# A hand-ordered drain for the last stage of a two-layer decoder, with the last softmax shares spread by TensorE and ScalarE

## The reference

```python
def _L1_xattn_ref(x, latents, mask, g1, b1, g2, b2, Wq, Wkv, Wout):
    xn, ln_lat = layer_norm(x, g1, b1), layer_norm(latents, g2, b2)
    q = ln_lat @ Wq
    k, v = jnp.split(jnp.concatenate([xn, ln_lat], axis=1) @ Wkv, 2, axis=-1)
    weight = einsum('bhld,bhnd->bhln', q * scale, k * scale)   # masked
    return to_rows(einsum('bhln,bhnd->bhld', softmax(weight), v)) @ Wout

def bitlinear(x, norm_w, w):
    x_norm = rmsnorm(x, norm_w)
    return einsum('bsd,hd->bsh', activation_quant(x_norm), weight_quant(w))

def _L1_ffn_ref(x, norm1_w, w1, act_scale, act_bias, norm2_w, w2):
    h = act_scale * square(relu(bitlinear(x, norm1_w, w1))) + act_bias
    return bitlinear(h, norm2_w, w2)

x = _layernorm(x + _L1_xattn_ref(ctx, x, mask, ...))
x = _layernorm(x + _L1_ffn_ref(x, ...))
```

## Time and profile before

| | us |
|---|---|
| median of 3 runs | 1576.4 |
| lowest, highest | 1575.58, 1577.85 |
| the profiled execution | 1580.26 |
| its span | 1578.4 |
| last score exponent (step 63) starts at | 1501.55 |
| TensorE busy over the span | 1415.3 (90%) |
| VectorE busy | 1132.3 (72%) |
| ScalarE busy | 959.6 (61%) |
| GpSimd busy | 306.6 (19%) |

### The profile page before, as it was taken

How to read it: one execution, slowest core, us unless ns; L and a number is a source line. 1 busy time by engine, 2 the same in 40 slices (tenths; PEclk the granted TensorE clock), 3 DMA queues, 4 the chain that set the end, 5 groups by cost and what they waited for, 6 DMA issues and landing times. The chain is left out here.

```text
span 1578.4 us, 32271 instructions
## 1 busy us (share of the span) xinstructions
PE 1415.3 (90%) x12643; PEld 868.5 (55%) x12658; DVE 1132.3 (72%) x2367; ACT 959.6 (61%) x1494; POOL 306.6 (19%) x278
## 2 busy tenths in 40 slices
PE   6999999998999888888898778999999999999962
PEld 4666666665665334434444354666666666666541
DVE  4666778885435799999999744455667767776787
ACT  2333367766555988899888843456555556555433
POOL 3433344542001101111010021121111111110011
PEclk9999999998999999999999999999999999999985
DMA  4000000000100000000000012222222222222310
GB/s 182 2 2 2 2 19 12 15 6 8 49 1 1 1 1 1 1 1 1 1 1 4 1 27 62 65 58 63 63 65 67 67 64 60 58 58 61 72 43 17
DMA packets 41013, 50.78 MB, mean 32 GB/s; under 512 B 9248, under 2 KB 23200, under 8 KB 40480
## 3 DMA queue, kind: packets, MB, share of 16 engines
q1 hardware_dynamic: 40576, 48.06, 11.9%
q10 hardware_dynamic: 288, 0.67, 0.1%
HBM read 13.04 MB, written 2.10 MB: 10 GB/s over the span
## 5 line engine op out<-in xcount | busy, mean ns | idle before, releaser
L1852 DVE TENSOR_TENSOR l_px<-psum,l_share 128x1024 f32<-128x1024 f32 x64 | 78.4, 1225 | 158.9 <-PE psum L1554 104.9
L1702 ACT ACTIVATE l_prob<-psum,l_bias 128x1024 f32<-128x1024 f32 x64 | 71.3, 1114 | 175.9 <-PE psum L1529 175.9
L1541 PE MATMUL psum<-l_XT,l_A 128*128 128x256 f32 x512 | 127.2, 393 | 1.5 <-ACT l_XT L1720 1.5
L1524 PE MATMUL psum<-l_th,l_XT 128*128 128x512 f32 x256 | 125.4, 613 | 1.5 <-DVE stream L1859 0.9
L1592 PE MATMUL psum<-l_px,l_N 128*128 128x256 f32 x512 | 124.8, 387 | 1.8 <-ACT l_r L1746 1.8
L1554 PE MATMUL psum<-l_prob,l_X 128*128 128x512 f32 x256 | 123.2, 604 | 0.0
L1592 PEld LDWEIGHTS psum<-l_px,l_N 128*128 128x128 f32 x512 | 94.6, 192 | 19.2 <-issue 4.7
L1833 DVE TENSOR_REDUCE l_top<-psum 128x8 bf16<-128x1024 f32 x64 | 78.1, 1221 | 36.4 <-PE psum L1609 36.4
L1541 PEld LDWEIGHTS psum<-l_XT,l_A 128*128 128x128 f32 x512 | 94.7, 194 | 12.6 <-ACT l_XT L1720 1.7
L1266 DVE TENSOR_TENSOR f_frac<-psum,f_whole 128x1024 f32<-128x1024 f32 x80 | 98.0, 1225 | 2.7
L1258 DVE TENSOR_SCALAR f_whole<-psum 128x1024 f32<-128x1024 f32 x80 | 97.5, 1218 | 1.6 <-PE psum L895 1.6
(11 more groups left out here) (310 smaller groups left out, 3216.2 us busy)
## 6 DMA issues: line engine op xcount, KB each, us to landing
l_share<-l_recip SPq DMA_DIRECT2D x512, 64.0 KB, 2.0
early_weights<-in_weights SPq DMA_DIRECT2D x1, 2405.0 KB, 11.4
c_cs<-in_ctx SPq DMA_DIRECT2D x16, 128.0 KB, 2.1
f_qf<-in_l_mats SPq DMA_DIRECT2D x1, 2048.0 KB, 8.0
out<-l_normed SPq DMA_DIRECT2D x16, 128.0 KB, 2.0
l_craw<-in_ctx SPq DMA_DIRECT2D x15, 128.0 KB, 2.3
late_weights<-in_weights SPq DMA_DIRECT2D x1, 1089.0 KB, 11.2
relbias<-in_relbias ACTq DMA_DIRECT2D x1, 512.0 KB, 5.2
```

Source lines behind the costliest of these rows:

```text
L1524: nc.tensor.matmul(ps[:, SC + n, :], XT[:, q % 3, k, :, :], th[:, q % 2, k, 8 * n:8 * n + 8, :], start=True, stop=False)
L1541: last = nc.tensor.matmul(ps[:, at + j // 2, (j % 2) * 256:(j % 2 + 1) * 256], A[:, QB * k + j, :], XT[:, q % 3, :, 1, :], start=True, sto ...
L1852: nc.vector.tensor_tensor(px[:, q % 2, :, k, :], ps[:, GA:GA + 2, :].rearrange("p a (h s) -> p (a h) s", s=S), share[:, (b // 2) % 2, b % ...
```

## The change

- Every engine's loop now stops at step 63 (`range(FIRST, B)`), and what followed is written as a list of calls, one quad at a time, in an order of its own on each engine.
- The last pair's shares (sequences 62 and 63) come no more by 16 DMAs. PE multiplies a column block of ones (`one_row`, one row of ones in each block of 32 partitions) by `recip`, four matmuls of 32 rows and 512 columns into banks 0 to 3 (`spread_last`), and ACT copies the banks into `share` (`keep_last_shares`).
- POOL's `normed_hidden` of quads 12 to 15 becomes a DVE product (`last_products`). DVE's `scaled_hidden` of these quads becomes an ACT pass (`last_scaled`). The two scale-and-add passes L1881 of the hidden values of quads 11 to 15 become two ACT passes (`last_lifted`). Quad 13's to 15's tokens keep theirs on DVE, but the tiny scale steps come apart from them.
- ACT's `measure` writes its unused squares into two idle buffers instead of `r`, so `r` is free sooner.
- Banks change: `hidden` of quads 13 to 15 goes to GA, the turned tokens to RO, the last quad's combine and turn-back to RO + 1, the gather of sequence 63 to RO. `deq2` has two copies.
- At the start of the phase DVE sets `one_row` with five memsets.

The core of the diff:

```diff
-            for i in range(FIRST, LAST):
+            for i in range(FIRST, B):
...
+            def spread_last():
+                pe.wait_ge(s["one_row"], 2)
+                pe.wait_ge(s["recip"], B // 2)
+                for n in range(4):
+                    rows = slice(32 * n, 32 * n + 32)
+                    last = nc.tensor.matmul(ps[:, (RO, RO + 1, SC, SC + 1)[n], :], one_row[rows, :], recip[rows, 1, :], start=True, stop=True)
+                last.then_inc(s["wide_ps"], 1)
...
+            def keep_last_shares():
+                act.wait_ge(s["wide_ps"], 1)
+                act.wait_ge(s["px_sb"], B - 4)
+                for b in range(2):
+                    at = (RO, SC)[b]
+                    nc.scalar.copy(share[:, 1, b, :, :], ps[:, at:at + 2, :]).then_inc(s["last_share"], 1)
...
+            def last_scaled(q):
+                act.wait_ge(s["squared"], q + 1)
+                act.wait_ge(s["hn"], q)
+                act.wait_ge(s["ss2"], q)
+                nc.scalar.activation(hh[:, :, :], r[:, :, :], ACT.Identity, scale=w("b_as"), bias=w("b_ab")).then_inc(s["hh"], 1)
+
+            def last_lifted(q):
+                act.wait_ge(s["hscaled"], q - OLD + 1)
+                for t in range(TQ):
+                    last = nc.scalar.activation(hn[:, t, :], hn[:, t, :], ACT.Copy, scale=hscale[:, t:t + 1], bias=MAGIC)
+                last.then_inc(s["hlifted"], 1)
...
+            def last_products(q):
+                dve.wait_ge(s["hh"], q + 1)
+                dve.wait_ge(s["q_ready"], q)
+                nc.vector.tensor_tensor(hn[:, :, :], hh[:, :, :], w("b_n2").unsqueeze(1).to_broadcast([P, TQ, HID]), ALU.mult
+                                        ).then_inc(s["hn"], 1)
...
+            def last_quantised(q):
+                dve.wait_ge(s["hlifted"], q - OLD + 1)
+                dve.wait_ge(s["q_ps"], TQ * q)
+                nc.vector.tensor_scalar(hi[:, :, :], hn[:, :, :], MAGIC, 127.0, ALU.subtract, ALU.min).then_inc(s["q_ready"], 1)
+                nc.vector.tensor_scalar(deq2[:, q % 2, :], amax2[:, :], 1.0 / 127.0, wmean[:, 1:2], ALU.mult, ALU.mult)
...
+            hidden_biggest(Q - 5)
+            divide(B - 3)
+            invert(B // 2 - 1)
+            last_scales(Q - 5)
+            tokens(Q - 3)
+            last_token_scales(Q - 3)
+            last_quantised(Q - 5)
+            divide(B - 2)
+            last_products(Q - 4)
...
```

More of the change, by code:

```diff
@@ new lines, in last_hidden_turned @@
+            def last_hidden_turned(q):
+                pe.wait_ge(s["q_ready"], q + 1)
+                pe.wait_ge(s["hiT_sb"], TQ * q)
+                pe.wait_ge(s["last_share"], 2)
+                for t in range(TQ):
+                    for n in range(HC):
+                        last = nc.tensor.matmul(ps[:, SC + t, n * P:(n + 1) * P], hi[:, t, n * P:(n + 1) * P], ident16[:, :],
+                                                start=True, stop=True)
+                    last.then_inc(s["q_ps"], 1)
@@ new lines, in last_down @@
+            def last_down(q):
+                pe.wait_ge(s["d_read"], q)
+                pe.wait_ge(s["sums_read"], B // 2)
+                down(q)
+            gather(B - 3)
+            pe.wait_ge(s["d_read"], Q - 5)
+            sums(B // 2 - 1)
+            hidden(Q - 4)
+            gather(B - 2)
+            pe.wait_ge(s["r_sb"], TQ * (Q - 3))
+            spread_last()
+            combine(Q - 2, 1)
+            combine(Q - 2, 2)
+            combine(Q - 2, 3)
+            gather(B - 1)
@@ new lines, in last_measure, with root1, root2 @@
+            def last_measure(q):
+                act.wait_ge(s["hh"], q + 1)
+                act.wait_ge(s["hscaled"], q - OLD)
+                act.wait_ge(s["staged"], Q - 1)
+                act.wait_ge(s["ss2"], q)
+                for t in range(TQ):
+                    last = nc.scalar.activation(junk[t], hh[:, t, :], ACT.Square, accum_out=ss2[:, t:t + 1])
+                last.then_inc(s["ss2"], 1)
+            def root1(q):
+                roots_of(q, None, None)
+            def root2(q):
+                roots_of(None, q, None)
@@ new lines, in last_tokens_quantised @@
+            def last_tokens_quantised(q):
+                dve.wait_ge(s["x_ps"], q)
+                for t in range(TQ):
+                    last = nc.vector.tensor_scalar(xn[:, t, :], xn[:, t, :], xscale[:, t:t + 1], MAGIC, ALU.mult, ALU.add)
+                step(last)
+                nc.vector.tensor_scalar(xi[:, :, :], xn[:, :, :], MAGIC, 127.0, ALU.subtract, ALU.min).then_inc(s["x_ready"], 1)
+                dve.wait_ge(s["r_sb"], TQ * q)
+                nc.vector.tensor_scalar(deq[:, :], amax[:, :], 1.0 / 127.0, wmean[:, 0:1], ALU.mult, ALU.mult).then_inc(s["deq1"], 1)
@@ new lines, in _ @@
+            divide(B - 2)
+            last_products(Q - 4)
+            hidden_biggest(Q - 4)
+            last_scales(Q - 4)
+            divide(B - 1)
+            last_tokens_quantised(Q - 3)
+            last_quantised(Q - 4)
+            last_residual(Q - 2)
+            residual_moments(Q - 2)
+            normalise(Q - 6)
+            tokens(Q - 2)
+            last_token_scales(Q - 2)
+            last_tokens_quantised(Q - 2)
+            last_products(Q - 3)
+            hidden_biggest(Q - 3)
@@ new lines, in _ @@
+            last_residual(Q - 1)
+            last_scales(Q - 3)
+            residual_moments(Q - 1)
+            down_read(Q - 5)
+            tokens(Q - 1)
+            last_token_scales(Q - 1)
+            last_tokens_quantised(Q - 1)
+            down_moments(Q - 5)
+            last_quantised(Q - 3)
+            last_products(Q - 2)
+            hidden_biggest(Q - 2)
+            normalise(Q - 5)
+            last_scales(Q - 2)
+            down_read(Q - 4)
+            down_moments(Q - 4)
```

197 lines of the change are left out of this document (179 added, 18 removed).

## The result

| | before | after |
|---|---|---|
| median, us | 1575.99 (4 runs, 1573.63 to 1577.85) | **1556.38** (4 runs, 1554.97 to 1560.69) |
| profiled execution, us | 1580.26 | 1560.69 |
| last score exponent starts at | 1501.55 | 1501.98 |
| last normalisation on DVE ends at | 1576.12 | 1556.60 |
| **drain**, the difference of these two | 74.57 | **54.62** |

The ratio of the times, estimated over all runs, is 0.9886, with a 95% interval of 0.9856 to 0.9916; the two medians alone give 0.9876. The profiled executions differ by 19.57 us and the medians by 19.61 (the profiled execution is one of the four runs after, but not one of the four before). The drain alone is 19.95 us shorter; it began 0.43 us later.

A forecast was written before the change was run, and what follows sets the result against it. DVE's 73.1 us queue after the last score bounds the drain: its 63.7 us of work becomes 53.1, plus 0.6 of waits, 19.4 us earlier. With 1.0 friction, net 18.4 less: median 1558.0, range 1555.5 to 1565.5.

The forecast's parts named there:

- A: Drain: DVE bounds it without gaps, each wait having a named cover; 1558.0 us, chance 0.70.
- POOL leaves: Drain, quads 10 to 13: DVE's normalisation passes fall from 2.66 to 0.60 us without POOL; 8.2 us less.
- The product: Drain: four hidden products come to DVE at 1.22 us plus 0.04 for the reduction's wait; 5.0 us more.
- Scaling and lifts: Drain: four scalings (2.9 us) and five quads' scale-and-add passes (4.5 us) leave DVE for ACT, hidden in its idle time.
- The spread: Last shares: four PE matmuls together take about 1.1 us, and DVE's 3.6 us wait for the DMAs goes.
- rival B: Mid-drain: PE falls to its lower clock and stays; 1564.7 us, or 1566.2 with the spread in turn; chance 0.20.
- Waits of 0.6 us for roots: End of drain: quads 14 and 15 each make DVE wait about 0.3 us for ACT's root.
- Friction: Drain: 1.0 us added for five margins below half a microsecond, at 0.2 us each.
- Tiny steps: DVE's drain: scale steps stay as many, quad 11's `hidden_biggest` only moves ahead of a `divide`; no effect.
- C: Drain: ACT becomes late from 12.6 us of added passes; 1559.8 us, or 1564.2 with slower lifts; chance 0.07.
- D: Drain: ACT's passes hold DVE as POOL's do, 28.4 us, making it slower at 1586.4 us; chance 0.01.
- E: Drain: no gain, from a new in-order block or table loads around ACT's roots; 1577.2 us at most; chance 0.02.

The follow-up runs named there:

- e1: Changed kernel with the hidden product of quads 12 to 15 back on POOL; drain 58.29 us (+3.67 to the change), median 1558.00 us.
- e12: Changed kernel with product on POOL, last shares by 16 DMAs, scaling and lifts on DVE, keeping order, banks, buffers; drain 68.60 us (-5.97 to before).
- e3: Changed kernel with scaling of quads 12 to 15 and lifts of quads 11 to 15 back on DVE; drain 62.34 us (+7.72 to the change).
- e2: Changed kernel with the last pair's shares by 16 DMAs again, without PE's spread and ACT's copies; drain 58.78 us (+4.16 to the change).
- e8: Changed kernel with one more unused 128x512 ACT pass before the scaling of each of quads 12 to 15; drain 56.17 us (+1.55).
- e2b: Changed kernel with last shares by DMA, plus 20 unread matmuls in PE's idle time; drain 57.05 us (+2.43 to the change).
- e4: Kernel before with only the hidden product of quads 12 to 15 moved to DVE, old order; drain 71.93 us (-2.64 to before).

## Why the prediction was right

Forecast 1558.0 with a range from 1555.5 to 1565.5; measured 1556.38. The case was A, a DVE queue almost without gaps. That the median came within 1.6 us is in part luck, since the start of the drain alone scatters by more; the drain's own length, below, is the better test. By the steps of the forecast:

- **POOL leaves, -8.2.** Right: every pair is at 0.60. But e1 and e12 show that the stretch would only have become a wait had the product stayed on POOL; that the product moves is what makes the term real.
- **The product, +5.0 at 1.22.** Right: 1223 ns, and 1.25 us from product to reduction. The choice of `divide` as the nearest row, with one operand in PSUM, held.
- **Scaling and lifts, -7.4.** Right: e3 gives 7.72. Their length on ACT was too small: 1.24 us for 1.06, 0.71 for 0.63, 13.5 us busy in all for 12.6 (the two lifts of a quad overlap a little, 1.32 us from start to end). The square of the earlier trace rows has no per-row operand; the scaling has two, the lift one. The Trainium skill (ScalarE: Activation LUTs, What ACT_TABLE_LOAD costs) gives 186 ns + 0.833 ns per element, and about 93 ns for each such operand. An estimate by that page is 1.225 and 0.706 us; the trace agrees, with 1.239 and 0.712, and the page would have been a better source than the nearest row.
- **The spread, 1.1 us, and the 3.6 us wait gone.** Right: 1.14, `divide` of 62 at 1511.93 for a forecast 1511.9. (The second estimate in the prediction is 3.5 / 3.07 = 1.14 us, not 1.2; nothing hangs on it.) That PE's clock hung on it as well (1.73 us in e2) was in rival B, as a danger, and not in the sum as a gain.
- **Waits of 0.6 us for roots.** Right: 0.5.
- **Friction, +1.0.** This term was mis-sized. The product of quad 13 comes just as its scaling ends (1524.54 + 1.24), for a margin forecast at 0.4, and DVE stands 0.19 us there and 0.06 us at each of the next two products: 0.3 us. The lifts of quads 13 to 15 end 0.07 to 0.15 us before DVE needs them. e8 shows that little more was left.
- **The sum.** Forecast for DVE's queue were 54.7 us; it took 53.15, from 1503.45 to 1556.60. 0.7 of the 1.5 us is the friction, 0.1 the roots. The other 0.7 is own work below the forecast 53.1. Most of it stands where the prediction had "Tiny steps. [...] Nothing". Before, the last scale step of the hidden values is followed by L1881, which needs its result:

```profile
1516.69 0.16 DVE L1879 TENSOR_TENSOR l_hscale<-l_hscale,l_ss 128x2 f32<-128x2 f32 x1
1516.89 0.88 DVE L1881 TENSOR_SCALAR l_hn<-l_hn,l_hscale 128x512 f32<-128x512 f32 x2
```

After, a step that does not need it comes next:

```profile
1508.36 0.16 DVE L2250 TENSOR_TENSOR l_hscale<-l_hscale,l_ss 128x2 f32<-128x2 f32 x1
1508.44 0.17 DVE L2090 RECIPROCAL l_roots<-l_roots 128x4 f32<-128x4 f32 x1
```

  From start to start that is 0.20 us before and 0.08 after, in each of the five quads: 0.6 us.

Rival B did not come. PE was idle for 1.17 and 1.20 us around the last combine, and the clock stayed at 1.00. The fall and what it costs were real, but at a gap of 4.86 us (e2), which the change itself removes. By the rule of the Trainium skill that B cited (TensorE: Matmul & The Clock Gate, A second HAM failure mode: psum-queue depth-cycling) frequent short idle times between groups of matmuls can make it swing; the two short ones in this trace did not. C was half right, ACT's passes being longer, but the margins held them. For D, the quantising pass L2255 takes 693 ns, as L1883 did before (0.69 us), beside 37.8 us of ACT work. (D's 28.4 us is a small slip: 0.88 of 32 us is 28.2. Nothing hangs on it.) E: one table load, no blocked queue.

## What to carry to other kernels

When the work of a loop runs dry, an order of its own for the drain pays by the waits that it removes from the busiest engine's queue (6.0 us here, e12). To forecast it, sum up that engine's queue, move passes off it to whatever has room, and count waits only where a producer is late. A pass given to a slow helper costs the bound engine its length if it is waited for, and can stretch a neighbouring pass by as much if it is not (2.1 to 2.5 us of DVE for each POOL pass here): compare that with the 1.2 us of doing it there. A gap in PE's work ahead of a burst of matmuls has a price beyond its length where it brings the clock down: here 4.86 us did, at 1.7 us on the end, and 1.2 us did not.

## What the runs showed of the hardware that was not expected

- The same ACT pass over 128x1024 takes 1.057 us as a square of the earlier trace rows and 1.239 us with a per-row scale and a per-row addend; over 128x512, 0.63 and 0.71.
- A gap of 4.86 us in PE's work brought the granted clock to 0.50 and nearly doubled the time of the next four heads, from 1.99 to 3.68 us, though PE was working again by then; 20 small matmuls in the gap prevented it (e2, e2b).
- The start of the drain lies up to 10.3 us apart in the profiles of kernels whose code ahead of it is nearly the same (8.93 us with the same code, before and e4), half of the whole change. Its cause was not looked for and stays open.
